# The head of a mixture-of-experts and GRU kernel, arranged anew with full-width products, and its gate inputs sent through memory group by group

## What is computed

```
shared = (silu(x @ w1) * (x @ w3)) @ w2
s      = sigmoid([x, cond] @ router_W);  top 2 of s + bias choose the experts, their s are normalized to gates
h[e]   = gelu(x @ W1e[e]);   routed = sum over e of gate[e] * (h[e] @ W2e[e])
x1     = x + (shared + routed) / 3
```

```
Z = sigmoid(x1 Wxz' + bxz + H Whz' + bhz);  R = sigmoid(x1 Wxr' + bxr + H Whr' + bhr)
Ht = tanh(x1 Wxh' + bxh + (R*H) Whh' + bhh);  H = Z*H + (1-Z)*Ht;  out = x1 + H Whq' + bhq
```

## Time and profile before

| | |
|---|---|
| median of 3 runs | 1314.22 us (1314.08 to 1318.01) |
| the profiled execution | 1317.0 us, of which the span from first to last instruction 1315.2 us |
| PE busy in the span | 1275.3 us (97%) |
| DVE, ACT, POOL busy | 1005.0, 799.5, 7.6 us |
| first product of the first GRU step | 74.67 us after the span's start |
| granted TensorE clock, mean | 0.997 |
| largest loads | W1e 2048 KB, W2e 2048 KB |

### The profile page before, as it was taken

How to read it: one execution, slowest core, us unless ns; L and a number is a source line. 1 busy time by engine, 2 the same in 40 slices (tenths; PEclk the granted TensorE clock), 3 DMA queues, 4 the chain that set the end, 5 groups by cost and what they waited for, 6 DMA issues and landing times.

```text
span 1315.2 us, 85216 instructions
## 1 busy us (share of the span) xinstructions
PE 1275.3 (97%) x36022; PEld 876.9 (67%) x36022; DVE 1005.0 (76%) x6121; ACT 799.5 (61%) x4384; POOL 7.6 (1%) x26
## 2 busy tenths in 40 slices
PE   8999999999999999999999999999999999999886
PEld 7667676767767676776767667666766767676443
DVE  3567878788787878778787877878787787877765
ACT  4156666666666666666666666666666666666554
POOL 1000000000000000000000000000000000000000
PEclk8999999999999999999999999999999999999999
DMA  8111112012111101211111121111111111010110
GB/s 266 33 45 22 48 23 43 25 30 51 25 50 23 42 25 30 50 25 49 23 39 30 30 51 24 50 21 37 33 30 44 25 43 30 18 38 14 44 20 11
DMA packets 79252, 51.39 MB, mean 39 GB/s; under 512 B 43032, under 2 KB 74264, under 8 KB 78872
## 3 DMA queue, kind: packets, MB, share of 16 engines
q1 hardware_dynamic: 78872, 45.95, 14.7%
HBM read 29.13 MB, written 16.78 MB: 35 GB/s over the span
## 4 chain that ended last, share of the span: by engine, by line
PE 88%; DVE 5%; ACT 3%; DMA 2%; issue 1%; SPq 0%
PE dn_ps L962 27%; PE up_ps L989 24%; PE zc_bank L1099 20%; PE r_bank L1099 14%; PE aux L962 2%; DVE terms L882 2%; DMA gru_raw<-gate_inputs_by_token 1%; ACT t_r L593 1%; DVE hist L885 1%; ACT t_h L613 1%; DVE t_rT L862 1%; PE misc L962 1%; DMA gate_inputs_by_token<-gru_raw 1%; DMA xT_all<-in_L_cond_w 1%; DVE factors L868 0%
## 5 line engine op out<-in xcount | busy, mean ns | idle before, releaser
L593 ACT ACTIVATE t_r<-r_bank 128x32 f32<-128x32 f32 x1024 | 146.2, 195 | 227.5 <-PE r_bank L1099 213.7
L962 PE MATMUL dn_ps<-we_sb,hid_e 128*32 128x256 f32 (+1 forms) x5176 | 281.3, 335 | 1.7 <-DVE x_all L748 1.2
L862 DVE STREAM_TRANSPOSE t_rT<-t_r 128x32 f32<-128x32 f32 x1024 | 156.0, 190 | 158.2 <-ACT t_r L593 148.8
L613 ACT ACTIVATE t_h<-zc_bank 128x32 f32<-128x32 f32 x1024 | 146.1, 195 | 210.2 <-PE zc_bank L1099 210.2
L1099 PEld LDWEIGHTS zc_bank<-whT,rhT 128*8 128x8 f32 x8192 | 119.1, 87 | 183.9 <-DVE rhT L865 179.9
L1099 PE MATMUL r_bank<-whT,hist 128*8 128x64 f32 x8192 | 212.2, 220 | 20.8 <-DVE hist L885 15.4
L1099 PE MATMUL zc_bank<-whT,rhT 128*8 128x64 f32 x8192 | 212.9, 220 | 4.7 <-issue 0.6
L1099 PE MATMUL zc_bank<-whT,hist 128*8 128x64 f32 x8192 | 209.8, 219 | 0.2 <-issue 0.2
L1099 PEld LDWEIGHTS r_bank<-whT,hist 128*8 128x8 f32 x8192 | 118.8, 88 | 125.9 <-DVE hist L885 99.9
L882 DVE STREAM_TRANSPOSE terms<-t_h 128x32 f32<-128x32 f32 x1024 | 156.8, 192 | 55.1 <-ACT t_h L613 20.0
L962 PEld LDWEIGHTS dn_ps<-we_sb,hid_e 128*32 128x32 f32 x5176 | 141.4, 110 | 37.8 <-DVE x_all L748 3.1
(11 more groups left out here) (114 smaller groups left out, 1664.0 us busy)
## 6 DMA issues: line engine op xcount, KB each, us to landing
gate_inputs_by_token<-gru_raw SPq DMA_DIRECT2D x32, 384.0 KB, 2.4
gru_raw<-gate_inputs_by_token SPq DMA_DIRECT2D x256, 48.0 KB
xT_all<-in_x SPq DMA_DIRECT2D x448, 8.0 KB
x_all<-in_x SPq DMA_DIRECT2D x32, 128.0 KB
out<-gru_raw SPq DMA_DIRECT2D x32, 128.0 KB
x_all<-in_L_cond_W1e SPq DMA_DIRECT2D x1, 2048.0 KB, 12.1
we_sb<-in_L_cond_W2e SPq DMA_DIRECT2D x1, 2048.0 KB, 13.0
xT_all<-in_L_cond_w SPq DMA_DIRECT2D x2, 512.0 KB, 6.2
```

The costliest lines, as they stand in the source:

```text
L593: act.activation(t_r[:, i, :], r_ps[:, i * Q:(i + 1) * Q], ACT.Tanh, scale=0.5).then_inc(tr_ready, 1)
L613: act.activation(t_h[:, i, :], c_ps[:, i * Q:(i + 1) * Q], ACT.Tanh, scale=-1.0).then_inc(th_ready, 1)
L862: dve.transpose(t_rT[:, i, :], t_r[:, i, :]).then_inc(trT_done, 1)
L962: done = pe.matmul(ps[Q * j:Q * (j + 1), col:col + cols], lhsT[:, Q * j:Q * (j + 1)], rhs, start=first, stop=last, tile_position=(0, Q * j ...
```

## The change

1. **Loads.** W1e is loaded in two parts (experts 0 and 1 right behind w3, the rest behind w2), W2e in two parts (two experts, six experts). w2 goes ahead of the rest of W1e, h0 behind everything but the biases. w1, w3 and the parts get semaphores of their own.
2. **Splits.** w1 and w3 are split in halves of their columns (four ACT copies and four DVE subtractions of 512 elements instead of two of 1024), and each of the first four units waits for its own part only. The splits of W1e are spread between the units. The 24 small routing operations on DVE are laid in two halves ahead of the first accumulations, and the copies of h0 go to a later round.
3. **Products of the head.** The `down`s and projections of the head use whole 128 x 128 weights (`full_product`) instead of four tiles of 32. The early logits go the other way, from whole to four tiles. In the 512 steps nothing is changed on PE.
4. **PE's order.** 16 instead of 10 products of zeros behind the first transposes; transposes of GRU weights one round later; `transpose_x1(0)` and `project(0, ...)` each 6 `up` matmuls earlier.
5. **Gate inputs.** The DRAM tensor is laid out by group, `[NG, P, RW]` instead of `[P, NG, RW]`. The store is cut into two, each issued when its half q is ready, and the gathers of a half wait only for its own store. This holds for all tiles.

```diff
-        by_token = nc.dram_tensor("gate_inputs_by_token", [P, NG, RW], F32, kind="Internal").ap()
+        by_group = nc.dram_tensor("gate_inputs_by_group", [NG, P, RW], F32, kind="Internal").ap()
...
-        ROUND_TR = [[], [("w", 0), ("w", 1)], [], [("w", 2), ("w", 3)], [("w", 4), ("w", 5)], [("w", 6)], [], []]
+        ROUND_TR = [[], [], [("w", 0), ("w", 1)], [("w", 2), ("w", 3)], [("w", 4), ("w", 5)], [("w", 6)], [], []]
+        FEW = 2
...
-            sp.dma_start(w1_raw, w1.rearrange("(k p) h -> p k h", p=P)).then_inc(ld_w13, 16)
-            sp.dma_start(w3_raw, w3.rearrange("(k p) h -> p k h", p=P)).then_inc(ld_w13, 16)
+            sp.dma_start(w1_raw, w1.rearrange("(k p) h -> p k h", p=P)).then_inc(ld_w13[0], 16)
+            sp.dma_start(w3_raw, w3.rearrange("(k p) h -> p k h", p=P)).then_inc(ld_w13[1], 16)
+            sp.dma_start(we1_raw[:, 0:FEW], we1[0:FEW].rearrange("e (k p) h -> p e k h", p=P)).then_inc(ld_we1[0], 16)
...
-            sp.dma_start(we1_raw, we1.rearrange("e (k p) h -> p e k h", p=P)).then_inc(ld_we1, 16)
+            sp.dma_start(w2_sb[:, :, :], w2.rearrange("(k p) c -> p k c", p=P)).then_inc(ld_w2, 16)
+            sp.dma_start(we1_raw[:, FEW:], we1[FEW:].rearrange("e (k p) h -> p e k h", p=P)).then_inc(ld_we1[1], 16)
+            for r, _, _ in WEIGHTS:
+                load_gru(r)
+            sp.dma_start(we2_sb[:, 0:FEW], we2[0:FEW].rearrange("e (k p) c -> p e k c", p=P)).then_inc(ld_we2[0], 16)
+            sp.dma_start(we2_sb[:, FEW:], we2[FEW:].rearrange("e (k p) c -> p e k c", p=P)).then_inc(ld_we2[1], 16)
...
-            def gate_rows(half, done):
-                for j in range(NG):
-                    src = by_token[:, j, :].rearrange("(b t) c -> b t c", b=B)[:, half * HALF:(half + 1) * HALF, :]
+            def store_inputs(t, q):
+                groups = slice(q * NG // PIECES, (q + 1) * NG // PIECES)
+                sp.wait_ge(xp_ready, PIECES * t + q + 1)
+                sp.dma_start(by_group[groups, :, :].rearrange("j p c -> p j c"), xproj[:, groups, :]).then_inc(xp_stored[q], 16)
+            def gate_rows(q, half, done):
+                for j in range(q * NG // PIECES, (q + 1) * NG // PIECES):
+                    src = by_group[j, :, :].rearrange("(b t) c -> b t c", b=B)[:, half * HALF:(half + 1) * HALF, :]
                     sp.dma_start(xs[Q * j:Q * j + B, half * HALF:(half + 1) * HALF, :], src).then_inc(done, 16)
...
-            sp.wait_ge(xp_ready, PIECES)
-            sp.dma_start(by_token, xproj[:, :, :]).then_inc(xp_stored, 16)
-            sp.wait_ge(xp_stored, 16)
+            for q in range(PIECES):
+                store_inputs(0, q)
             sp.wait_ge(xs_zeroed, 1)
-            gate_rows(0, xs_first)
-            gate_rows(1, xs_second)
+            for q in range(PIECES):
+                sp.wait_ge(xp_stored[q], 16)
+                gate_rows(q, 0, xs_first)
+            for q in range(PIECES):
+                gate_rows(q, 1, xs_second)
...
+            def full_product(ps, cols, lhsT, rhs, first, last):
+                return pe.matmul(ps[:, 0:cols], lhsT, rhs, start=first, stop=last, skip_group_check=True)
...
+                if p == 0 and place < NSH and m % (3 * KC) == 0:
+                    pe.wait_ge(w13_split, 2 * (place // 2) + half + 1)
...
-                        pe.matmul(misc[:, i * NE:(i + 1) * NE], xT_all[:, i, k, :], rw_sb[:, k, :], start=(k == 0), stop=(k == KC - 1))
+                        last = product(misc, i * NE, NE, xT_all[:, i, k, :], rw_sb[:, k, :], k == 0, k == KC - 1)
...
-                for k in range(NSH if g == 0 else HE // P):
-                    down(t, g, k)
+                for k in range(chunks_of(g)):
+                    down(t, g, k, full=True)
...
-            warm(10)
+            warm(16)
...
-            for m in range(UP_MM):
+            for m in range(UP_MM // 2):
                 up(1, m)
             transpose_x1(0)
-            for m in range(UP_MM, UP_MM + UP_MM // 2):
+            for m in range(UP_MM // 2, UP_MM):
                 up(1, m)
             for q in range(PIECES):
                 for k in range(KC):
-                    project(0, q, k)
+                    project(0, q, k, full=True)
...
-                    project(1, *PROJ1[r][1:])
+                    project(1, *PROJ1[r][1:], full=True)
```

More of the change, by code:

```diff
@@ L150, in moe_then_gru @@
         ld_bias = sem("ld_bias")
-        ld_w13 = sem("ld_w13")
+        ld_w13 = [sem(f"ld_w13_{i}") for i in range(2)]
         ld_w2 = sem("ld_w2")
-        ld_we1 = sem("ld_we1")
-        ld_we2 = sem("ld_we2")
+        ld_we1 = [sem(f"ld_we1_{i}") for i in range(2)]
+        ld_we2 = [sem(f"ld_we2_{i}") for i in range(2)]
         ident0 = sem("ident0")
@@ L182, in moe_then_gru @@
         xp_ready = sem("xp_ready")
-        xp_stored = sem("xp_stored")
+        xp_stored = [sem(f"xp_stored{q}") for q in range(2)]
         xs_first = sem("xs_first")
@@ L563, in _ @@
             take(2)
+            split_we1(0)
             consume_up(0, 2)
-            split_we1(0)
+            split_we1(1)
             consume_up(0, 3)
[L567 to L570, removed]
+            split_we1(2)
+            score_tanh(0, slice(0, EARLY))
             for e in range(NE):
+                if e + 3 < NE:
+                    split_we1(e + 3)
                 consume_up(0, NSH + e)
@@ L806, in _ @@
             split_we1(2)
-            split_we1(3)
[L808 to L818, removed]
+            ops = route(slice(0, EARLY))
+            for op in ops[:len(ops) // 2]:
+                op()
+            accumulate(0, 0)
+            for op in ops[len(ops) // 2:]:
+                op()
+            accumulate(1, 0)
+            split_we1(3)
             for e in range(2, NE):
+                if e + 2 < NE:
+                    split_we1(e + 2)
                 take_round(e)
@@ L824, in _ @@
                     gate_biases()
+                if e == 5:
+                    dve.wait_ge(ld_h0, 16 * NG)
+                    link(dve.transpose(h0T[:, :, :].rearrange("p i q -> p (i q)"), h0_rows[:, :, :].rearrange("p i q -> p (i q)")))
+                    for i in range(NI):
+                        dve.tensor_copy(hist[:, TS - 1, i, :, 1], h0T[:, i, 0:B]).then_inc(hT_ready, 1)
                 if e == NE - 2:
@@ L830, in _ @@
             copy_x1T(0)
+            shared(1, 0)
             for q in range(PIECES):
@@ L833, in _ @@
             accumulate(1, NE)
-            for u in HEAD_UNITS:
+            for u in HEAD_UNITS[1:]:
                 shared(1, u)
@@ L943, in early_logits @@
                 pe.wait_ge(tr_dve, 1)
+                for k in range(KC):
+                    product(misc, NT * NE, NE, condT[:, k, :], rw_sb[:, KC + k, :], k == 0, k == KC - 1)
                 for i in range(EARLY):
                     for k in range(KC):
-                        pe.matmul(misc[:, i * NE:(i + 1) * NE], xT_all[:, i, k, :], rw_sb[:, k, :], start=(k == 0), stop=(k == KC - 1))
-                for k in range(KC):
-                    last = pe.matmul(misc[:, NT * NE:(NT + 1) * NE], condT[:, k, :], rw_sb[:, KC + k, :], start=(k == 0), stop=(k == KC - 1))
+                        last = product(misc, i * NE, NE, xT_all[:, i, k, :], rw_sb[:, k, :], k == 0, k == KC - 1)
                 last.then_inc(logits_done, 1)
@@ L972, in up @@
                         pe.wait_ge(x_split, p + 1)
-                    if p == 0 and place == 0:
-                        pe.wait_ge(w13_split, 2)
                     if p == 0 and u >= 0:
@@ L992, in up, with down @@
                     done.then_inc(up_done, 1)
-            def down(t, g, k, begin=0, end=2):
+            def full_product(ps, cols, lhsT, rhs, first, last):
+                return pe.matmul(ps[:, 0:cols], lhsT, rhs, start=first, stop=last, skip_group_check=True)
+            def down(t, g, k, begin=0, end=2, full=False):
                 cols = slice((t % 2) * P, (t % 2 + 1) * P)
@@ L1015, in down @@
                     lhsT, w = hid_e[:, (g - 1) % HRING, k, cols], we2_sb[:, g - 1, k, :]
-                done = product(dn_ps[t % 2], begin * P, (end - begin) * P, lhsT, w[:, begin * P:end * P], k == 0 and begin == 0, k == chunks_of(g) - 1)
+                if full:
+                    done = full_product(dn_ps[t % 2], C, lhsT, w, k == 0, k == chunks_of(g) - 1)
+                else:
+                    done = product(dn_ps[t % 2], begin * P, (end - begin) * P, lhsT, w[:, begin * P:end * P],
+                                   k == 0 and begin == 0, k == chunks_of(g) - 1)
                 if k == chunks_of(g) - 1 and end == 2:
@@ L1031, in transpose_x1, with project @@
                 done.then_inc(x1T_done, 1)
-            def project(t, q, k):
+            def project(t, q, k, full=False):
                 if k == 0:
@@ L1146, in _ @@
                 for k in range(KC):
-                    project(0, q, k)
-            for m in range(UP_MM + UP_MM // 2, 2 * UP_MM):
```

(2 more changed lines are left out.)

61 lines of the change are left out of this document (31 added, 30 removed).

## The result

The changed kernel takes 1297.99 us (median of 4 runs, 1297.48 to 1298.8), the kernel before 1315.16 us (4 runs, 1314.08 to 1318.01): ratio 0.986, 95% interval 0.9844 to 0.9876. That is 17 us less, where I had forecast 11 and a range that ended at 1299.5. Measured twice more, the same code came to ratios of 0.9879 (0.9864 to 0.9894) and 0.9871 (0.9851 to 0.989), 16.1 and 16.5 us less by the medians.

A forecast was written before the change was run, and what follows sets the result against it. PE was taken to bound the kernel, with nearly all of the gain in the first 74.67 us: 10.5 us less there plus 0.8 within the steps, 11.3 in all, from 1314.2 to 1303.0 us; range 1299.5 to 1308.5.

The forecast's parts named there:

- Start, clock and logits: In the head: first unit 2.5 us earlier, full clock at the start 1.75 less, early logits 1.1 less.
- the second slow stretch: Clock at about half behind the early logits, 24.1 to 29.1 us; 1.5 us less without it.
- Full width: Whole products in the head's downs: fewer changes between up and tiles, 1.0 us less, ends 2.2 less and 1.5 more.
- T: End of tile 0's last down (group 8) in the head, forecast at 52.2 us against 60.72 before.
- the hand-over: From the end of tile 0's last down to the first step: waits for hid and gathered inputs go, 1.95 us less.
- Routing and loads: In the head: earlier routing on DVE ends PE's wait, 1.2 us less; W2e's first part late, 0.5 charged.
- The first rival: Loads hold PE in the head, which loses 3 to 5 us: 1306 to 1308; chance 0.13.
- Within the steps: Every second tile's gathers: half stored two steps earlier, two gathers behind the last store; 0.8 us less, ends 0 and 3.
- my third rival: Split store makes gathers late for ACT's seed_r at the 15 even tiles: slower, 1318; chance 0.05 for slower or same.
- The whole-product rival: In the head's whole products, weight load and streaming take turns: 8 us lost, 1311; chance 0.06.
- deeper gain: Case of a larger gain than the forecast's own range of 1300.5 to 1306; chance 0.06.
- My fourth rival: Head falls shorter than summed, DVE or ACT its bound; other way 1295 to 1299 with whole products at 2.2, W2e in time.

The follow-up runs named there:

- whole_logits: The changed kernel with the early logits as whole 128-wide products again; ratio 0.9879 to the kernel before.
- tiled_products: The changed kernel with four column tiles again in the head's downs and projections; ratio 0.9897 to the kernel before.
- warm10: The changed kernel with 10 instead of 16 products of zeros ahead of the first unit; ratio 0.987 to the kernel before.

## Why the prediction was wrong

1. **Start, clock and logits:** right, each within 0.25 us (the second slow stretch, 1.5 forecast, gave 0.63 in the unit and 0.84 in the `down`), and whole_logits shows the mechanism that I had only inferred from the second slow stretch.
2. **Full width, the first step that failed:** a mis-sized term. I had "0.05 for each of 15 expert downs and 0.1 for the two shared ones", 1.0 us, with 2.2 as the end. The rate of a whole record was right (0.216 from start to start, 4.32 us for 20), though my 0.24 rested on a misreading: the zeros' 0.122 is the length of the row by its count, from start to start it is 0.112. What I priced wrongly was the change of shape. I charged it to the `down`s alone. There it is 1.3 us between the two kernels, not far from my 1.0. Another 1.5 stands in what follows a `down`: six units at 1.41 instead of 1.56 to 1.62, and three transposes at 0.44 instead of 0.59. The seventh unit, which followed a transpose in the kernel before, was 1.41 already. That is 2.8 us before T, beyond my end of 2.2. Of the 0.9 that the hand-over gave beyond my 1.95, 0.6 is the same thing (11.6 us from T in tiled_products, 11.05 in the changed kernel). Undone in the new head it costs about 4, and 0.9 to 1.4 more for the wait inside the first down.
3. **Routing and loads:** right in kind. The rest of W1e landed at 9.64 + 10.8 = 20.4 (forecast 21.0), W2e's first part at 19.26 + 7.9 = 27.2 (27 to 29). PE waited 0.05 there, and its first `down` took 1.10 instead of 0.87: 0.3 in all, not 0.5. The first rival, loads that hold PE, missed by little: in warm10 PE waits 0.83 us at this place.
4. **Hand-over:** the mechanism was right. PE's last projection and the inputs (60.88) arrive together. From T to the first step it took 11.05, where I had 12.0; most of the difference is in item 2.
5. **Within the steps, the second step that failed and the larger miss:** I took 0.8 with 3 as the end, from a single wait of 1.3 that the list of waits showed, and the steps gave 3.7 by the medians. The delay at the seam is spread: one store costs 2.0 to 5.3 us over 16 seams, and the split store next to nothing. I had the place and the mechanism, and my third rival even named the seam, but only as a danger. I did not add up the 16 gaps in the trace before, which would have given 2.0. The rest of the 3.7 isn't assigned: it lies within what the medians and the scattered stalls leave open.
6. **The whole-product rival** (load and stream in turn) is wrong: 0.216 a record.
7. **The range:** its low end, 1299.5, took the terms one at a time; the result lies 1.5 below it, and either of items 2 and 5 priced rightly would have brought it inside. Terms that erred to the same side were the "deeper gain" to which I gave 0.06. My fourth rival gave 1295 to 1299 for whole products at 2.2 and W2e in time, but these two come to 1.7 us, 1301.3; its bound, DVE or ACT in the head, didn't appear, and the 1298 came from elsewhere.

## What to carry to other kernels

A change of tiling shape on PE is paid by the neighbour too (here 1.5 us of 2.8): compare the length of the same work behind a product of the same and of another shape before you price a form. When a transfer is due on every second tile, add up the gaps at that place over the whole trace; here the list of waits showed one of 1.3 us where the gaps summed to 2.0. One edit's worth depends on what stands next in line: whole products gave nothing measurable where w2 and the routing were late and about 4 us where they were not, so a head is to be costed with all its edits in place.

## What was unexpected

- TensorE's clock fell to 0.5 without any idle stretch, behind 2.1 us of matmuls with 8 columns (twice: before, and whole_logits), and not behind 0.79 us of them.
- A `down` in column tiles stood still inside itself, after its 17th record, for 0.94 and 1.39 us, with the DMA engines at a share of 1.08 and 1.09 and no releaser shown. The whole form, with a quarter of the matmuls, did not.
- Scattered stalls in the 512 steps differ from execution to execution, 0.3 to 6.2 us in 17 profiles. Their cause stays open.
